# Attention weights in the masks of the sums, made by an exponential per visit on ScalarE

## The reference, cut to what matters

```python
def _gat_relation(x, src, dst, mask, N, Wr, a_src, a_dst, br):
    h = x @ Wr
    s = h @ a_src
    d = h @ a_dst
    e = jax.nn.leaky_relu(s[src] + d[dst], negative_slope=NEG_SLOPE)
    e = jnp.where(mask, e, -jnp.inf)
    m = jax.ops.segment_max(e, dst, num_segments=N)
    w = jnp.where(mask, jnp.exp(e - m[dst]), 0.0)
    denom = jax.ops.segment_sum(w, dst, num_segments=N)
    alpha = w / denom[dst]
    msg = alpha[:, None] * h[src]
    return jax.ops.segment_sum(msg, dst, num_segments=N) + br
...
for r in range(R):
    mask = jnp.concatenate([edge_type == r, ones_loops])
    out = out + _gat_relation(x, src, dst, mask, N, W[r], att_src[r], att_dst[r], bias[r])
```

## Time and profile before

| | us |
|---|---|
| median of 3 runs | 4082.32 |
| lowest and highest | 4075.14, 4087.51 |
| profiled execution | 4076.66 |
| its span in the profile | 4074.7 |
| attention stage, first to last top (L1029) | 275.1 to 1878.1 |

### The profile page before, as it was taken

How to read it: one execution, slowest core, us unless ns; L and a number is a source line. 1 busy time by engine, 2 the same in 40 slices (tenths; PEclk the granted TensorE clock), 3 DMA queues, 4 the chain that set the end, 5 groups by cost and what they waited for, 6 DMA issues and landing times. The chain is left out here.

```text
span 4074.7 us, 77799 instructions
## 1 busy us (share of the span) xinstructions
PE 2867.3 (70%) x16134; PEld 2008.6 (49%) x16135; DVE 2338.2 (57%) x8613; ACT 1459.4 (36%) x3275; POOL 2325.4 (57%) x1835
## 2 busy tenths in 40 slices
PE   1627677777767677656779959887878787777752
PEld 1315455555555555444334436666666566666631
DVE  7138888888888888776342244444444444444423
ACT  0115555454455455443000004333333333333320
POOL 0046676666666666550000006888888888888880
PEclk9955555555555565556879978888888989898976
DMA  1354334333433333784614304555555555555543
GB/s 45 101 111 118 96 105 116 105 105 107 115 102 105 110 105 105 84 103 110 206 49 124 98 13 51 53 54 53 54 54 54 54 53 54 53 54 54 54 41 77
DMA packets 651838, 336.52 MB, mean 83 GB/s; under 512 B 436752, under 2 KB 612163, under 8 KB 650820
## 3 DMA queue, kind: packets, MB, share of 16 engines
q0 software_dynamic: 148736, 86.57, 22.1%
q1 hardware_dynamic: 453094, 119.03, 13.8%
q10 hardware_dynamic: 49824, 129.15, 8.3%
HBM read 156.42 MB, written 202.84 MB: 88 GB/s over the span
## 5 line engine op out<-in xcount | busy, mean ns | idle before, releaser
L2129 POOL DMA_INDIRECT sums<-el_rows,el_idx x816 | 1269.1, 1555 | 648.0 <-DVE el_rows L2343 399.3
L830 POOL DMA_INDIRECT at_hs<-table,at_rec_s x976 | 1048.7, 1074 | 586.7 <-issue 289.0
L971 PE MATMUL near_ps<-at_pair_hot,at_src_low_hot 128*128 128x425 f16 x976 | 498.9, 511 | 461.6 <-ACT at_count_s L868 273.3
L868 ACT CAST at_count_s<-near_ps 128x400 f16<-128x400 f32 x976 | 481.9, 494 | 874.4 <-PE near_ps L971 423.2
L2341 DVE CAST el_idx<-el_place 128x4 uint32<-128x4 f32 x204 | 35.5, 174 | 843.3 <-DMA sums<-el_rows,el_idx 795.3
L943 PEld LDWEIGHTS sums_ps<-at_hw,at_hit 128*128 128x128 f32 x1952 | 471.3, 333 | 34.1 <-issue 28.9
L943 PE MATMUL sums_ps<-at_hw,at_hit 128*128 128x66 f32 x1952 | 442.3, 408 | 8.3 <-DVE acc L1017 8.3
L971 PEld LDWEIGHTS near_ps<-at_pair_hot,at_src_low_hot 128*128 128x128 f16 x976 | 129.1, 132 | 601.1 <-ACT at_count_s L868 339.5
L1009 DVE TENSOR_SCALAR at_pair_hot<-iota_wide,at_rec_s 128x400 f16<-128x400 f16 x976 | 320.8, 331 | 1.9
L2277 ACT ACTIVATE el_h<-el_h_ps,el_valid 128x128 f32<-128x128 f32 x816 | 232.6, 368 | 237.9 <-PE el_h_ps L2191 166.6
L2145 PE MATMUL el_miss_t<-ident_b,el_miss 128*128 128x128 bf16 x816 | 83.7, 264 | 312.6 <-DVE el_miss L2315 312.6
(11 more groups left out here) (355 smaller groups left out, 5127.1 us busy)
## 6 DMA issues: line engine op xcount, KB each, us to landing
slots<-at_count_s ACTq DMA_DIRECT2D x122, 850.0 KB
el_rec<-attr SPq DMA_DIRECT2D x816, 32.0 KB
chunk<-slots SPq DMA_DIRECT2D x240, 100.0 KB
attr<-in_edge_attr SPq DMA_DIRECT2D x19, 1248.0 KB
chunk<-slots ACTq DMA_DIRECT2D x224, 100.0 KB
at_rec_s<-meta SPq DMA_DIRECT2D x992, 3.5 KB
at_hs<-table,at_rec_s POOLq DMA_INDIRECT x976
el_pair<-meta SPq DMA_DIRECT2D x816, 1.0 KB
```

The lines of the kernel that those rows point to most:

```text
L830: pool.indirect_dma_start(hs[:, s, u, :], None, k.table, bass.IndirectOffsetOnAxis(rec[:, s, u, 0:1].bitcast(U32), 0)).then_inc(gathered[s ...
L868: a.copy(count[:, (n.o + d) % 2, i, 0:AW], near[:, (n.o + d) % 2, 0:AW]).then_inc(count_ready, 1)
L971: pe.matmul(near[:, s, 0:SW], low_hot[:, s, i, :], pair_hot[:, s, i, :], start=False, stop=True, skip_group_check=(i > 0)).then_inc(near_r ...
L2129: pool.indirect_dma_start(k.sums_flat[a], bass.IndirectOffsetOnAxis(idx[:, j, a:a + 1], 0), rows[:, j, a, :], None, compute_op=ALU.add).th ...
```

## The change

The mask of the sums is no longer 0/1. `hit` becomes exp(far x 2^-88 + lz): at an edge's own key `far` is the score, which 2^-88 makes vanish, so that exp(lz) is left, the weight; elsewhere the argument is about -4096, and the exponential is 0. As the bias lz is one value per edge and visit, each visit needs an instruction of its own: eight of 128 x 128 for a batch, in pairs between the copies. They work on the batch that the small exponential worked on (n - 1), while the masks before were made for batch n; so `far` is kept longer and gets a third buffer. The tiles `weight` and `hw` go, VectorE's product too, and the sums take `hs` as gathered. GpSimd, which frees a place of `hs` for the next gather, waits for the sums instead of the product; TensorE waits for the exponentials alone.

```diff
--- before.py
+++ after.py
@@ -719,7 +719,7 @@
         hs = sb("hs", [P, RING, B, TW])
         key = sb("key", [P, 2, 2, B])
         miss = sb("miss", [P, 2, B, P])
-        far = sb("far", [P, 2, B, P])
+        far = sb("far", [P, 3, B, P])
         low_hot = sb("src_low_hot", [P, 2, B, P], F16)
         pair_hot = sb("pair_hot", [P, 2, B, SW], F16)
         count = sb("count_s", [P, 2, B + 1, SW], F16)
@@ -737,8 +737,6 @@
         fade = sb("fade", [P, 3, B])
         zed = sb("zed", [P, 2, B])
         lz = sb("lz", [P, 2, B])
-        weight = sb("weight", [P, 2, B])
-        hw = sb("hw", [P, 2, B, TW])
         masked = ps("masked", [P, B, P])
         picked = ps("picked", [P, CW])
         sums = ps("sums_ps", [P, 2, CW])
@@ -754,8 +752,7 @@
                                                           sem("fade_ready"))
         pick_ready, picked_ready, zed_taken, weight_asked = (sem("pick_ready"), sem("picked_ready"), sem("zed_taken"),
                                                              sem("weight_asked"))
-        weight_ready, hw_ready, sums_ready, acc_step = (sem("weight_ready"), sem("hw_ready"), sem("sums_ready"),
-                                                        sem("acc_step"))
+        sums_ready, acc_step = sem("sums_ready"), sem("acc_step")
         near_ready, count_ready, count_written = (sem("near_ready"), sem("count_ready"),
                                                   [sem("count_written0"), sem("count_written1")])
         deg_added, dst_copied = sem("deg_added"), sem("dst_copied")
@@ -820,7 +817,7 @@
                 pool.wait_ge(rec_loaded[s], (n.round(0) + 1) * (16 * B))
                 if n.after(RING):
 
-                    pool.wait_ge(hw_ready, n(1, 1 - RING))
+                    pool.wait_ge(sums_ready, n(1, 1 - RING))
                 pool.sem_inc(passed, 1)
                 for u in range(B):
                     if n.after(LEAD):
@@ -850,15 +847,17 @@
                 a.activation(hit_t[:, s, half], masked[:, half], ACT.Identity, bias=k.ones_f[:, 0:1],
                              scale=1.0 / BIG).then_inc(hit_t_ready, 1)
 
-            def hits(n, h):
-
-                s, half = n.o % 2, slice(4 * h, 4 * h + 4)
-                if h == 0:
-                    act.wait_ge(far_ready, n(1, 1))
-                    if n.after(2):
-                        act.wait_ge(sums_ready, n(1, -1))
-                a.activation(hit[:, s, half], far[:, s, half], ACT.Identity, bias=k.ones_f[:, 0:1],
-                             scale=1.0 / BIG).then_inc(hit_ready, 1)
+            def weights(n, d, i):
+
+                s, m = (n.o + d) % 2, (n.o + d) % 3
+                if i == 0:
+                    act.wait_ge(weight_asked, n(1, d + 1))
+                    if n.after(2 - d):
+                        act.wait_ge(sums_ready, n(1, d - 1))
+                for u in (2 * i, 2 * i + 1):
+                    w = a.activation(hit[:, s, u], far[:, m, u], ACT.Exp, bias=lz[:, s, u:u + 1], scale=2.0 ** -88)
+                if i == 3:
+                    w.then_inc(hit_ready, 1)
 
             def keep(n, d, i):
 
@@ -878,21 +877,22 @@
                     keep(n, 1, 0)
                     keep(n, 1, 1)
                 if n.has(-1):
-                    act.wait_ge(weight_asked, n(1))
-                    a.activation(weight[:, (n.o + 1) % 2], lz[:, (n.o + 1) % 2], ACT.Exp).then_inc(weight_ready, 1)
+                    weights(n, -1, 0)
                 if n.has(1):
                     keep(n, 1, 2)
-                if n.has(0):
-                    hits(n, 0)
+                if n.has(-1):
+                    weights(n, -1, 1)
                 if n.has(1):
                     keep(n, 1, 3)
+                if n.has(-1):
+                    weights(n, -1, 2)
                 if n.has(0):
                     act.wait_ge(fade_asked, n(1, 1))
                     a.activation(fade[:, n.o % 3], fade_in[:, n.o % 2], ACT.Exp).then_inc(fade_ready, 1)
                 if n.has(1):
                     keep(n, 1, 4)
-                if n.has(0):
-                    hits(n, 1)
+                if n.has(-1):
+                    weights(n, -1, 3)
                 if n.has(1):
                     keep(n, 1, 5)
                     turned(n, 1, 0)
@@ -912,7 +912,7 @@
                     if n.after(1 - d):
                         pe.wait_ge(top_ready, n(1, d))
                 for u in range(4 * h, 4 * h + 4):
-                    t = pe.transpose(masked[:, u, :], far[:, (n.o + d) % 2, u, :], k.ident[:])
+                    t = pe.transpose(masked[:, u, :], far[:, (n.o + d) % 3, u, :], k.ident[:])
                 t.then_inc(masked_ready, 1)
 
             def picks(n, h):
@@ -934,13 +934,12 @@
 
                 s = (n.o + d) % 2
                 if h == 0:
-                    pe.wait_ge(hw_ready, n(1, d + 1))
-                    pe.wait_ge(hit_ready, n(2, 2 * d + 2))
+                    pe.wait_ge(hit_ready, n(1, d + 1))
                     if n.after(1 - d):
 
                         pe.wait_ge(acc_step, n(B, d * B))
                 for u in range(4 * h, 4 * h + 4):
-                    m = pe.matmul(sums[:, u // 4, (u % 4) * TW:(u % 4 + 1) * TW], hit[:, s, u, :], hw[:, s, u, :],
+                    m = pe.matmul(sums[:, u // 4, (u % 4) * TW:(u % 4 + 1) * TW], hit[:, s, u, :], hs[:, (n.o + d) % RING, u, :],
                                   start=True, stop=True)
                 if h == 1:
                     m.then_inc(sums_ready, 1)
@@ -1031,9 +1030,9 @@
                     q = (n.o + 1) % RING
                     dve.wait_ge(gathered[q], (n.round(1) + 1) * (16 * B))
                     dve.wait_ge(key_step, n(2, 4))
-                    if n.after(1):
-                        dve.wait_ge(hit_ready, n(2))
-                    v.scalar_tensor_tensor(far[:, w], miss[:, w], -BIG, hs[:, q, :, D + 1:D + 2].to_broadcast([P, B, P]),
+                    if n.after(2):
+                        dve.wait_ge(hit_ready, n(1, -1))
+                    v.scalar_tensor_tensor(far[:, (n.o + 1) % 3], miss[:, w], -BIG, hs[:, q, :, D + 1:D + 2].to_broadcast([P, B, P]),
                                            ALU.mult, ALU.add).then_inc(far_ready, 1)
                 if back:
                     dve.wait_ge(picked_ready, n(1))
@@ -1117,10 +1116,6 @@
                         ins = pairs(n, 2, u)
                         if u == B - 1:
                             ins.then_inc(hot_ready, 1)
-                    if back and u == 3:
-                        dve.wait_ge(weight_ready, n(1))
-                        v.tensor_tensor(hw[:, w], hs[:, (n.o - 1) % RING],
-                                        weight[:, w].unsqueeze(2).to_broadcast([P, B, TW]), ALU.mult).then_inc(hw_ready, 1)
 
             v.memset(k.zero_f[:], 0.0).then_inc(run_start, 1)
             v.memset(run[:, 1, B:B + 1], -BIG).then_inc(run_start, 1)
```

## The result

The changed kernel takes 4212.5 us (median of 4 runs), the kernel before 4078.7: ratio 1.032, interval 1.028 to 1.036. One of the four runs, 4336.9 us, had a lower granted clock (0.65 against 0.75) and is left out of the ratio. The forecast was 4057 us in a range of 4028 to 4094, so the time lies outside, on the other side. The profiled execution has a span of 4202.3 us. All of the loss stands in the attention stage.

What follows compares the result with a forecast made beforehand. The prediction took the chain of count matmul on TensorE and count copy on ScalarE as the bound; -5 - 25 + 5 + 0 = -25 us led from the median 4082.3 to 4057 us, range 4028 to 4094.

Steps and rivals of the forecast that it cites:

- What bounds the kernel: Attention stage: the chain of count matmul on TensorE and count copy on ScalarE sets the end in nearly all rounds.
- VectorE's product: Dropping it shortens VectorE's batch by 0.61 us: -5 us where count matmuls wait for VectorE, -25 us from earlier pair masks.
- the first rival: VectorE's saving ends as idleness, 60 to 70 us more ahead of its top; 4082 us, chance 0.30.
- lead and round length: Lead: how long VectorE's last pair mask precedes the previous batch's last count copy; 2 us or more went with 11 us rounds.
- the prediction's own sum: Rounds timed from the later of last pair mask and previous batch's last count copy to the second `hit_t` half's end.
- ScalarE's pairs: Exponentials in pairs between count copies, 0.62 us a pair, lengthen 25 rounds at the upper clock by 0.18 us: +5 us.
- the third rival: Exponential pairs on ScalarE lengthen the count and copy chain by 0.2 us a batch: 4101 us, chance 0.10.
- Waits that move: Moved waits on TensorE, VectorE and GpSimd, whose first gather comes 2 to 3 us later, cost nothing: 0 us.
- late rounds: Slower rival: five short rounds behind the loop's head, where VectorE is late, lose their shortness: +11 us, 4093 us, chance 0.05.

Runs made afterwards that it cites:

- before_gate_sums: The kernel before with one wait changed: GpSimd's first gather of a batch waits for the sums of six batches back, not the product; ratio 1.024 (1.022 to 1.026).
- after_no_gathers: The changed kernel without gathers behind the first six batches, later batches working on stale rows; ratio 0.944 (0.942 to 0.946) of the kernel before.
- shift4_tick: The changed kernel with gathers waiting for counts four visits later, plus a 128x32 memset that GpSimd waits for behind every gather; ratio 1.097 (1.095 to 1.099).

## Why the prediction was wrong

**What bounds the kernel** was right: the chain of count and copy, and VectorE's product lies off it.

**VectorE's product**, -5 and -25 us: sized right and put to the wrong account. The stretch from top to last pair mask became 0.6 us shorter. Its worth shows where the gathers don't interfere more than before, in the changed kernel with gathers four visits later: ratio 0.998, and VectorE's idleness ahead of the top is, by the groups of that kernel,

```profile
L1028 DVE TENSOR_REDUCE at_top<-masked 128x8 f32<-128x1024 f32 x122 | 149.4, 1224 | 228.1 <-issue 125.5 <-ACT at_hit_t L847 102.5
```

and the count's weight load waits for the pair mask, by its waits,

```profile
PEld near_ps L970 <- DVE at_pair_hot L1008: 1.1, 3, 0.6
```

228 us instead of 171 in before, 57 more, nearly the 60 to 70 that the first rival had named as its sign; the waits for pair masks fell from 11.5 us to 1.1. So lead and round length have no tie that VectorE could use. In the same kernel, by the prediction's own sum, leads of 2 us and more did become more frequent, 48 of 113 rounds instead of 31 of 103, but these rounds took 11.9 us instead of 11.0, and the mean stayed. The -25 us were not there. The first rival (saving ends as idleness, 4082) would have been right of the change less its gate.

**ScalarE's pairs**, +5 us: right in kind. One exponential takes 397 ns (estimated 411; by the Trainium skill, "ScalarE: Activation LUTs", section "What ACT_TABLE_LOAD costs", an estimate of 280 + 128 x 0.833 = 387, with which the row agrees within 3%), a pair 0.69 us where 0.62 was taken, so the next starts after 0.30. Between the fourth and the fifth copy of a round the distance at the upper clock (where the count matmul takes 0.35 us, and not 0.56) grew from 0.94 to 1.08 us, in 29 rounds of the stage: 29 x 0.14 = 4 us. At the lower clock it stayed 1.21, so the third rival, pairs in the chain, didn't come about, and its time, 4101, would have been too low as well.

**Waits that move** is the step that failed. It said of GpSimd's first gather that it comes "some 2 to 3 us later", took 0 because GpSimd idles 4.5 us a batch and its rows come two batches early, and gave no bound above. The gather came 3.8 us later (5.7 against 1.9). The 4.5 us of idleness were misread: the 0.30 us that stand ahead of every gather of a row are in them, 951 x 0.30 = 285 of the 548 us, so GpSimd waited only 2.2 us a batch and works for the other 11. The slack was smaller than the shift, and the gate began to bind. That the rows come early does hold: in neither kernel, nor in the one with the gate alone, did VectorE wait for rows. But the price isn't paid by who waits for the rows. With the gate binding, TensorE's counts come late more often and by more, above all at the second visit of a batch (0.7 us of lateness a batch before, 1.4 after) and the seventh (0.4 and 1.0). In place of 0 stand about 2.4% of the program (before_gate_sums against its own before), 98 us of the 134 on this kernel's scale. The rest, 0.8%, isn't the exponentials, since the kernel before without the product has it too (1.035); whether it is the missing product or the sums' reading of `hs` isn't shown. It appears only together with the gate, since with the gathers held two to six visits later the whole change is worth -0.2 to +0.1%. None of the rivals had this mechanism: the slow side had pairs and late rounds.

**A version that beats both**: the changed kernel with each gather waiting for a count four visits later, 4069.7 us against 4078.1 of the kernel before beside it, ratio 0.998 (0.997 to 0.999), and 3.3% below the changed kernel. It is the change as it was meant, with one number more.

**Open** remain: why TensorE's signal comes late while gathers go out (whether the matmul ends late or its signal travels late, the trace can't tell, since matmul ends are modelled); whether the issue on GpSimd or the gathers' transfers do it; and how a binding gate makes it worse. That the gate costs 2.4% is shown by an edit of one wait, and that gathers make copies late by leaving them out. The way from the one to the other is not: longer runs account for about 0.2 of the 1.4 us a batch, and three to five gathers in a run cost 0.61 us a copy in after and 0.19 in before.

## What to carry to other kernels

An engine's idleness is no slack for a wait that is moved. First take out of it the short gaps that stand between any two of its instructions; then ask whether a gate that was always open will now bind, and what the engine's work does to others. When a row names a wait "remote", don't explain it by what goes along with it (here the lead, and SyncE's slow loads) before the candidates have been left out one by one. And when an experiment takes a loss away, look whether another engine has become the bound or the gate has stopped binding before you credit the edit. Here it was best to hold each gather by a wait of its own, and not to let eight in by one gate and leave GpSimd to catch up.

## What the runs showed of the hardware

While GpSimd issues indirect DMAs back to back (mostly 0.95 us each, 1.06 to 1.08 on average, 0.30 between), what waits for TensorE's matmuls starts up to 4.9 us late, though nothing in the program ties the two: 134 of 874 copies in after, 114 of 929 in before, none in after_no_gathers once the last gather is out, and none of 744 in shift4_tick, with 0.95 us between any two gathers. The changed kernel without gathers takes 5.6% less than the kernel before. A memset of 128x32 on GpSimd that is waited for makes 0.95 us of the 0.30 between two gathers, where its row has 0.14. Two and four raises of a semaphore there leave the distance of 1.25 us inside a row of gathers as it is, though the program takes 0.6 and 1.0% more.
